# Reordering the hand-over between the two phases of a fused two-layer gated cross-attention kernel on Trainium2

## The reference

```
x = x + tanh(g_xattn[0]) * quantised_matmul(layernorm(x), ctx)           # fp8 steps, context as the weight
x = x + tanh(g_ffn[0])   * ternary_ffn(layernorm(x), W0, gamma)           # RMS norm, 8-bit activations, ternary W0
x = x + tanh(g_xattn[1]) * attention(layernorm(x), ctx, ctx)              # 8 heads of 128 rows per batch, softmax over 1024
x = x + tanh(g_ffn[1])   * mixture(layernorm(x), router_w, Wa, Wb)        # 8 experts of rank 128, the best 2
```

```
scale = max(max(abs(rms_norm(x) * gamma)), 1e-5);  q = round(clip(x / scale * 127, -128, 127))
```

## Time and profile before

| | before |
|---|---|
| median of 3 runs | 2047.13 us (2046.15 to 2052.06) |
| the profiled execution | 2047.11 us, span 2045.3 us |
| granted TensorE clock, mean | 0.982 of full speed |
| TensorE busy | 1859.9 us (91%) |
| VectorE busy | 1542.8 us (75%) |
| ScalarE busy | 1269.0 us (62%) |
| GpSimd busy | 775.0 us (38%) |
| DMA moved | 340.50 MB, mean 166 GB/s |

### The profile page before, as it was taken

How to read it: one execution, slowest core, us unless ns; L and a number is a source line. 1 busy time by engine, 2 the same in 40 slices (tenths; PEclk the granted TensorE clock), 3 DMA queues, 4 the chain that set the end, 5 groups by cost and what they waited for, 6 DMA issues and landing times.

```text
span 2045.3 us, 26459 instructions
## 1 busy us (share of the span) xinstructions
PE 1859.9 (91%) x8968; PEld 838.5 (41%) x8968; DVE 1542.8 (75%) x2386; ACT 1269.0 (62%) x2045; POOL 775.0 (38%) x1100
## 2 busy tenths in 40 slices
PE   1699999983799999999999999999999999999998
PEld 0244444331244444444444444444444444444443
DVE  8899999887777777777777777777777777777662
ACT  4799898655555665665665555665656565565650
POOL 3556565333333333333333333333333333333320
PEclk9999999997799999999999999999999999999998
DMA  9587877795788788888878888788878878887672
GB/s 212 159 213 200 217 208 186 187 233 167 143 157 161 149 164 167 163 159 168 160 159 167 164 163 159 150 167 162 159 161 164 169 157 161 163 171 160 125 147 58
DMA packets 923975, 340.50 MB, mean 166 GB/s; under 512 B 849728, under 2 KB 898880, under 8 KB 923840
## 3 DMA queue, kind: packets, MB, share of 16 engines
q1 hardware_dynamic: 923840, 338.81, 78.8%
HBM read 93.36 MB, written 33.55 MB: 62 GB/s over the span
## 4 chain that ended last, share of the span: by engine, by line
DVE 21%; ACT 20%; issue 19%; POOL 10%; PE 7%; DMA 5%; SPq 1%; ACTq 0%; DVEq 0%; POOLq 0%
ACT slot L881 9%; DVE tiny L1570 7%; ACT arena L868 6%; POOL tiny L707 5%; DVE tiny L1216 4%; POOL tiny L705 4%; DVE slot L1575 3%; ACT tiny L860 3%; DMA slot<-slot 2%; DVE arena L1585 2%; DMA probs<-slot 2%; ACT slot L905 2%; DVE slot L1543 2%; PE accs L1059 1%; PE accs L1060 1%
## 5 line engine op out<-in xcount | busy, mean ns | idle before, releaser
L1575 DVE SCALAR_TENSOR_TENSOR slot<-arena,tiny,slot 128x1024 f16<-128x1024 f32 x256 | 328.2, 1283 | 304.2 <-ACT slot L881 304.0
L881 ACT ACTIVATE slot<-arena,tiny 128x1024 f16<-128x1024 f32 x256 | 294.2, 1149 | 173.1 <-POOL tiny L707 158.1
L1079 PE MATMUL sc<-arena,slot 128*128 128x512 f16 x1536 | 372.3, 382 | 20.9 <-ACT arena L868 18.5
L705 POOL TENSOR_SCALAR tiny<-tiny 128x1 f32<-128x1 f32 x256 | 101.0, 394 | 687.0 <-ACT arena L868 687.0
L1570 DVE TENSOR_REDUCE tiny<-sc 128x1 f32<-128x1024 f32 x256 | 306.6, 1207 | 17.5 <-PE sc L1079 16.2
L868 ACT ACTIVATE arena<-sc,tiny,head_tab 128x1024 f32<-128x1024 f32 x256 | 308.6, 1205 | 8.5
L860 ACT ACTIVATE tiny<-tiny,head_tab 128x1 f32<-128x1 f32 x256 | 74.3, 290 | 346.0 <-DVE tiny L1570 346.0
L1079 PEld LDWEIGHTS sc<-arena,slot 128*128 128x128 f16 x1536 | 150.2, 98 | 207.2 <-ACT arena L868 21.2
L1100 PE MATMUL accs<-probs,arena 128*128 128x512 f16 x512 | 195.9, 383 | 18.9 <-issue 16.4
L1059 PE MATMUL accs<-wa_both,slot 128*128 128x512 f16 x512 | 196.6, 384 | 0.0
L1060 PE MATMUL accs<-wa_both,slot 128*128 128x512 f16 x512 | 196.6, 384 | 0.0
(11 more groups left out here) (212 smaller groups left out, 2902.9 us busy)
## 6 DMA issues: line engine op xcount, KB each, us to landing
arena<-in_x SPq DMA_DIRECT2D x32, 512.0 KB, 4.2
x_scratch<-arena SPq DMA_DIRECT2D x32, 512.0 KB, 3.7
slot<-x_scratch SPq DMA_DIRECT2D x32, 512.0 KB, 4.0
slot<-in_ctx SPq DMA_DIRECT2D x32, 512.0 KB, 4.2
out<-arena SPq DMA_DIRECT2D x31, 512.0 KB, 3.4
slot<-in_L_ffn_Wa SPq DMA_DIRECT2D x12, 512.0 KB, 4.7
slot<-in_L_ffn_Wb SPq DMA_DIRECT2D x9, 512.0 KB, 5.0
wb_hi<-in_ctx SPq DMA_DIRECT2D x64, 64.0 KB, 2.4
```

The source lines that it names most:

```text
L881: act.activation(high, full, ACT.Identity, scale=rinv[c % 4][:]).then_inc(s_ph.sem, 1)
L1079: mm = pe.matmul(sc[:, c % 2, h * HALF:(h + 1) * HALF], q[i][:, c * P:(c + 1) * P], k[j][:, h * HALF:(h + 1) * HALF], start=start, stop=stop)
L1575: dve.scalar_tensor_tensor(out=low, in0=full, scalar=rinv[c % 4][:], in1=high, op0=ALU.mult, op1=ALU.subtract).then_inc(s_pl.sem, 1)
```

## The change

It alters only the hand-over and the prologue.

- SyncE, step j = 31: after the x1 loads it loads context tile 0 as well, waits for the store of tile 29, and loads Wb 0 to 2; at j = 32, behind W0's last transpose, Wb 3 to 5. The stores of x1 tiles 30 and 31 leave the loop.
- SyncE after `go`: quantised tiles 0 and 1 are transposed first, then Wb 6 and 7, context tile 1, the stores of tiles 30 and 31, and the chunks. Key 0 is transposed after chunk 1 (behind a wait for all x1 stores), quantised tile 2 after chunk 5, and context tile 2 is loaded after chunk 6.
- ScalarE makes key 0's high part before `go`, ahead of six Wb tiles; Wb 6 and 7 come after the query of tile 0, key 1's high part after chunk 4.
- VectorE does the mean and gamma of tile 0 (`quantise_norm(0)`) before `x1_max(31)`; after `go` only the scaling (`quantise_scale(0)`) is left. Both quantised tiles are rounded before key 0's low part. Wb 3 comes before the first row maximum, Wb 6 and 7 at chunks 2 and 3, quantised tile 2 at chunks 4 and 5, key 1 at chunk 6, Wb 4 and 5 later in turn 1.
- Two Wb tiles have other landing places: Wb 4 lies in the upper part of `wb_lo` that its own low halves fill later, Wb 5 in slot 4; Wb 6 and 7 stay in the array of probabilities.

```diff
@@ -141,8 +141,8 @@
         C = [ring[:, i] for ring in rings for i in range(4)][:C_RING - 1] + [slot[4][:]]
         CQ = lo_hi(rings[2][:, 3])
         RAW = ((slot[11][:], slot[12][:]), (rings[2][:, 2], rings[2][:, 3]))
-        WB_RAW = [XP[25 % X_RING], XP[26 % X_RING], XP[27 % X_RING], XS, slot[4][:]]
-        WB_RAW += [quarters(probs[:].bitcast(F32))[:, i] for i in range(5, KB)]
+        WB_RAW = [XP[25 % X_RING], XP[26 % X_RING], XP[27 % X_RING], XS, rings[2][:, 2], slot[4][:]]
+        WB_RAW += [quarters(probs[:].bitcast(F32))[:, i] for i in range(6, KB)]
 
         def raw(kind, r):
 
@@ -429,16 +429,18 @@
                 if PREP < j <= PREP + KB:
                     turn_w0(j - PREP - 1)
                 if j == TILES - 1:
-                    sp.wait_ge(x1_out.sem, x1_out.at(TILES - 3))
+                    sp.wait_ge(x_q.sem, x_q.at(TILES - 1))
                     for n in range(3):
                         sp.dma_start(X2[n][:], rows(x1_rows, n)).then_inc(xa_in[n].sem, 16)
+                    sp.dma_start(KX[:], rows(c_rows, 0)).then_inc(kx_in.sem, 16)
+                    sp.wait_ge(x1_out.sem, x1_out.at(TILES - 3))
+                    sp.wait_ge(e_sq.sem, e_sq.at(TILES - 5))
+                    for r in range(3):
+                        load_wb(r)
                 if j == TILES:
-                    sp.wait_ge(x1_out.sem, x1_out.at(TILES - 2))
-                    sp.wait_ge(e_sq.sem, e_sq.at(TILES - 2))
-                    sp.wait_ge(x_q.sem, x_q.at(TILES - 1))
-                    for r in range(5):
+                    for r in range(3, 6):
                         load_wb(r)
-                if is_x(j - 1):
+                if is_x(j - 1) and j < TILES - 1:
                     store_x1(j - 1)
                 if SUM_FROM - 1 <= j < SUM_FROM + KB:
                     load_sum(j - SUM_FROM + 1)
@@ -447,11 +449,6 @@
                 if PREP + 1 <= j < PREP - 1 + KB:
                     load_prep(j - PREP + 1)
 
-            sp.wait_ge(x1_out.sem, x1_out.at(TILES - 1))
-            sp.dma_start(KX[:], rows(c_rows, 0)).then_inc(kx_in.sem, 16)
-            sp.wait_ge(mm1.sem, mm1.at(TILES - 1))
-            for r in range(5, KB):
-                load_wb(r)
             sp.wait_ge(go.sem, 1)
 
 
@@ -519,14 +516,20 @@
                 sp.dma_start_transpose(blocks(HT), T42).then_inc(h_turned.sem, 16)
 
             turn_quantised(0)
+            turn_quantised(1)
+            for r in range(6, KB):
+                load_wb(r)
             load_k(1)
-            turn_quantised(1)
-            turn_keys(0)
+            for n in range(TILES - 2, TILES):
+                store_x1(n)
             for c in range(KB - 1):
                 turn_probs(0, c)
                 if c == 1:
-                    load_k(2)
-            turn_quantised(2)
+                    sp.wait_ge(x1_out.sem, x1_out.at(TILES - 1))
+                    turn_keys(0)
+                if c == 5:
+                    turn_quantised(2)
+            load_k(2)
             for n in range(1, TILES + 2):
                 before, prev, cur, nxt, quant = (is_x(n + d) for d in (-2, -1, 0, 1, 2))
                 if prev:
@@ -799,6 +802,10 @@
                 act.wait_ge(wp_in[r % 2].sem, wp_in[r % 2].at(r // 2))
                 act.activation(raw(0, r), raw(0, r), ACT.Identity, scale=winv[:]).then_inc(w_n.sem, 1)
                 act.activation(wa_hi[:, r, :], raw(1, r), ACT.Identity, scale=wamp[:, 0:1]).then_inc(wa_hi_set.sem, 1)
+
+            def key_high(n):
+                act.wait_ge(kx_in.sem, kx_in.at(n))
+                act.activation(KHL[n % 2][0], KX[:], ACT.Identity, scale=head_tab[:, n, 0:1]).then_inc(k_hi.sem, 1)
 
             def output_high(r):
                 act.wait_ge(wb_in[r].sem, wb_in[r].at(0))
@@ -847,13 +854,10 @@
                 if is_x(j - 1) and j < PREP:
                     x1_square(j - 1)
 
-            for r in range(5):
+            key_high(0)
+            for r in range(6):
                 output_high(r)
             act.wait_ge(go.sem, 1)
-
-            def key_high(n):
-                act.wait_ge(kx_in.sem, kx_in.at(n))
-                act.activation(KHL[n % 2][0], KX[:], ACT.Identity, scale=head_tab[:, n, 0:1]).then_inc(k_hi.sem, 1)
 
             def exp(n, c):
                 act.wait_ge(s_mx.sem, s_mx.at(n, c + 1))
@@ -919,12 +923,10 @@
                 act.wait_ge(m_turned.sem, m_turned.at(n))
                 act.copy(T4HL[0][:, half], T4[:, half]).then_inc(h_hi.sem, 1)
 
-            key_high(0)
-            for r in range(5, KB):
-                output_high(r)
-            key_high(1)
             for h in range(2):
                 query_half(0, h)
+            for r in range(6, KB):
+                output_high(r)
             exp(0, 0)
             for c in range(1, KB):
                 exp(0, c)
@@ -933,6 +935,8 @@
                     query_full(1)
                 if c == 2:
                     query_high(1)
+                if c == 4:
+                    key_high(1)
             prob_high(0, KB - 1)
             for n in range(1, TILES + 1):
                 prev, cur, nxt = (is_x(n + d) for d in (-1, 0, 1))
@@ -1422,6 +1426,26 @@
                 x_mask(n)
                 x_step(n)
                 x_add(n)
+
+            def quantise_norm(n):
+                dve.wait_ge(xa_in[n % 3].sem, xa_in[n % 3].at(n // 3))
+                if n == 0:
+                    dve.wait_ge(x_hi.sem, x_hi.at(TILES - 1))
+                    dve.wait_ge(x_lo.sem, x_lo.at(TILES - 1))
+                    dve.wait_ge(gamma_in.sem, gamma_in.at(0))
+                if n > 1:
+                    dve.wait_ge(l3_lo.sem, l3_lo.at(n - 1))
+                dve.scalar_tensor_tensor(out=Y[n == 1][:], in0=X2[n % 3][:], scalar=row_tab[:, n, 0:1], in1=gamma_b[:],
+                                         op0=ALU.add, op1=ALU.mult).then_inc(s2_y.sem, 1)
+
+            def quantise_scale(n):
+                y = Y[n == 1]
+                dve.wait_ge(s2_y.sem, s2_y.at(n, 1))
+                dve.tensor_scalar(y[:], y[:], row_tab[:, n, 1:2], ROUND_INT, ALU.mult, ALU.add).then_inc(s2_y.sem, 1)
+
+            def quantise_full(n):
+                quantise_norm(n)
+                quantise_scale(n)
 
             dve.wait_ge(ids.sem, 4)
             dve.tensor_reduce(own_block.rearrange("p (n k) -> p n k", k=KB),
@@ -1474,6 +1498,8 @@
                     round_x(j + 2)
                 if is_x(j + 4) and j + 4 >= X_EARLY:
                     x_stats(j + 4)
+                if j == TILES + 1:
+                    quantise_norm(0)
                 if is_x(j - 2):
                     if j == 2:
                         dve.wait_ge(gsq.sem, 1)
@@ -1520,16 +1546,6 @@
             dve.wait_ge(w_turned.sem, w_turned.at(KB - 1))
             dve.tensor_copy(gmax[:], gq[:]).then_inc(go.sem, 1)
 
-            def quantise_full(n):
-                y = Y[n == 1]
-                dve.wait_ge(xa_in[n % 3].sem, xa_in[n % 3].at(n // 3))
-                if n != 1:
-                    after(dve, l3_lo, n - 1)
-                dve.scalar_tensor_tensor(out=y[:], in0=X2[n % 3][:], scalar=row_tab[:, n, 0:1], in1=gamma_b[:],
-                                         op0=ALU.add, op1=ALU.mult).then_inc(s2_y.sem, 1)
-                dve.wait_ge(s2_y.sem, s2_y.at(n, 1))
-                dve.tensor_scalar(y[:], y[:], row_tab[:, n, 1:2], ROUND_INT, ALU.mult, ALU.add).then_inc(s2_y.sem, 1)
-
             def quantise_round(n):
                 dve.wait_ge(s2_y.sem, s2_y.at(n, 2))
                 if n != 1:
@@ -1645,31 +1661,31 @@
                 dve.scalar_tensor_tensor(out=x[:, cols], in0=accs[:, bank, :], scalar=ocol[:], in1=x[:, cols],
                                          op0=ALU.mult, op1=ALU.add).then_inc(o_x4.sem, 1)
 
-            quantise_full(0)
+            quantise_scale(0)
             quantise_round(0)
             quantise_full(1)
+            quantise_round(1)
             key_low(0)
-            quantise_round(1)
             for r in range(2):
                 output_low(r)
             for h in range(2):
                 finish_x2_half(0, h)
             output_low(2)
             finish_x2(1)
+            output_low(3)
             row_maxima(0, 0)
             row_maxima(0, 1)
-            output_low(3)
             for c in range(2, KB):
                 row_maxima(0, c)
                 prob_low(0, c - 2)
-                if c == 2:
+                if c < 4:
+                    output_low(c + 4)
+                if c == 4:
+                    quantise_full(2)
+                if c == 5:
+                    quantise_round(2)
+                if c == 6:
                     key_low(1)
-                if 3 <= c < 6:
-                    output_low(c + 2)
-                if c == 6:
-                    quantise_full(2)
-                if c == 7:
-                    quantise_round(2)
             prob_low(0, KB - 2)
             for n in range(1, TILES + 2):
```

(6 more changed lines are left out.)

## The result

Over five runs the changed kernel took 2032.83 us in the median (2028.76 to 2035.89), the kernel before 2046.15 (2044.05 to 2052.06) in the same rounds: ratio 0.9928 with a 95% interval of 0.991 to 0.9946, **13.3 us faster**. The profiled execution took 2032.83 us, span 2031.0. Of the changed kernel's nine runs (these five and the four of "The changed kernel again") three took 2028.28 to 2029.48 us at a mean granted clock of 0.990, and six 2032.83 to 2036.23 us at 0.987; both profiles of it are from the six.

What follows compares the result with a forecast made beforehand. Bound: the chain of waits between the phases, before a loop of 46.9 us turns where TensorE is nearly always busy. 9.1 - 0.4 + 3.1 + 2.6 = 14.4 us off 2047.1 gives 2032.7 us; 8-in-10 range 2028.5 to 2040.

Steps and rivals of the forecast that it cites:

- Landing of tile 0's transpose: SyncE's queue before product 0: issued at 467.05, landing at 471.4 instead of 480.47, 9.1 us earlier; bounds 7 and 10.
- The bound "empty queue": Upper bound for tile 0's transpose: with nothing queued ahead it lands at 470.97 or a little faster, 10 us gained.
- The first exponential, 0.4 late: ScalarE, tile 0: Wb 6 and 7, about 1.1 us each, into 1.83 us of idle, delay it by 0.4 us.
- Leg 2: Chunks of tile 0: tile 2's earlier transpose starts product 2 3.1 us earlier, the kept clock saves 2.6; bounds 0 and 6.5.
- leg 1: Hand-over before product 0: tile 0's transpose no longer waits for tile 31's store and lands 9.1 us earlier.
- "the clock falls 2 us after the last matmul": TensorE before product 2: the idle dropped the clock to 1.2 GHz; without it 16 matmuls take 3.47, not 6.11 us.
- "What is late next": Second half of tile 0's values: TensorE waits about 1 us for chunk 7, ends at 537.8; VectorE needs it from 539.9.
- A (a gap stays ahead of product 2): Tile 2's transpose lands over 2 us after the scores, the clock falls; gain 9 to 12 us, 2035 to 2038; chance 0.27.
- B (late scale): W0's last transpose, behind seven loads, lands at 467 to 468, delaying the scale 1.6 to 2.5 us: 2035; chance 0.1.
- C (worse rhythm): Loop: turns settle slower at the router's wait; 0.46 us more a turn eats the gain, 0.7 gives 2054; chance 0.04.
- D: Before tile 0's transpose: the wait only changes place, leaving under 6 us of gain, 2041 to 2047; chance 0.05.
- E: Loop: fewer turns over 46.9 us; a third less of 9.5 us of excess gives 2029.5; chance 0.06.

Runs made afterwards that it cites:

- The changed kernel again: The changed kernel run once more with nothing altered: 2034.66 us, ratio 0.994 (0.9917 to 0.9962), hand-over 87.4 us.
- Late mean: The changed kernel with tile 0's mean and gamma (1.28 us) put back behind the scale: one time of 2037.38 us, hand-over 87.2 us.
- the run with the stores first and no wait: The changed kernel with x1 tiles 30 and 31 stored inside the loop again, no wait before tile 0's transpose: 2036.29 us, hand-over 88.8 us.
- The run with extra matmuls: The changed kernel with matmuls whose results are overwritten unread, put where TensorE idles: 2027.74 us, ratio 0.9915 (0.9899 to 0.9932), hand-over 82.8 us.
- leg 2 only: The kernel before with only tile 2 quantised at chunks 4 and 5 and transposed after chunk 5: 2042.48 us, ratio 0.9981, hand-over 99.5 us.
- leg 1 only: The changed kernel with tile 2's quantising and transpose, key 1 and context tile 2 at their old places: 2035.05 us, ratio 0.9944, hand-over 88.7 us.
- late tile 2: The changed kernel with SyncE transposing quantised tile 2 after chunk 6 instead of after chunk 5: one time of 2032.52 us, hand-over 87.11 us.
- context tile 2 early: The changed kernel with context tile 2 loaded after chunk 4's transpose instead of after chunk 6's: one time of 2037.34 us, hand-over 86.15 us.
- before with extra matmuls: The kernel before with matmuls whose results are overwritten unread in its own idle stretches: 2043.49 us, ratio 0.9982 (0.9969 to 0.9995), hand-over 100.25 us.

## Why the prediction was right, step by step

The forecast was 14.4 us and 2032.7; measured are 13.3 us of hand-over, 14.3 of span and 13.3 in the medians. The span has 0.33 us from a phase one that ended earlier and 0.68 from the loop and the end, which is within what single executions differ by there. The mechanism is the one forecast: both gates were where I had put them, and both opened. That the sum comes so close is luck in part, because its errors cancel:

| step of the prediction | forecast | measured | from |
|---|---|---|---|
| tile 0's transpose lands, product 0 starts earlier | 9.1 | 10.3 | 22.88 - 12.55 |
| from product 0 to the first row maximum | -0.4 | -1.8 | 12.58 against 14.38 |
| product 2 starts earlier, from the first row maximum | 3.1 | 3.7 | 36.75 against 33.08 |
| product 2 at the high clock | 2.6 | 2.65 | 6.21 against 3.56 |
| from the add on product 2 to the router | 0 | -1.6 | 21.99 against 23.55 |

*Landing of tile 0's transpose: mis-sized by 1.2 us.* The issue was right: 6.0 us earlier, counted from the last add, against 6.1. The landing behind it took 3.06 us and not the 4.35 that I had from the full queue's pace of 1.55 us a load (471.4 - 467.05). In the changed kernel Wb 3 to 5 landed about 1.25 us apart, and the engines had nothing left to move from 466.8. Late mean shows the other side: one instruction of 1.28 us more before the issue, product 0 later by 1.4. Why the pace of before was slower stays open. A store at its end is not enough: in the run with the stores first and no wait, Wb 4 and 5 landed 1.3 us apart with a store behind them. The bound "empty queue" was the right value.

*The first exponential, 0.4 late: wrong in its cause, and the way there is 1.8 longer.* Wb 6 and 7 took ScalarE 2.18 us and were finished 0.7 us before the row maximum was. What came late was TensorE: products 0 and 1 started at the low clock and kept it longer than before (9.42 against 8.62 us), and then the first scores ran at it too (4.42 against 3.05). I had counted the clock where it falls in the kernel before, and not where it might newly fall in the changed one. The run with extra matmuls has 7.08 and 3.05 us there.

*Leg 2: right in place and in size up to product 2, but not at the router.* The gate was the transpose of tile 2, the clock followed, and the add on product 2 came 6.3 us earlier against 5.7. At the router, counted from the first row maximum, leg 2 alone shows 3.6 us and the whole change 4.8; put on top of leg 1, it shortened the hand-over by 1.6 us. I had split the sum into 8.7 and 5.7 us, and leg 1 alone gave 11.7. But "the clock falls 2 us after the last matmul" does not hold: late tile 2 kept it across 2.56.

*"What is late next": wrong in its size, and the largest error.* I wrote that TensorE waits a microsecond for chunk 7 and that VectorE does not want `values(0, 1)` yet. TensorE waited 2.77 us, the clock then fell and the product took 7.0 us, and VectorE idled 1.46 us for it. Chunk 7's transpose was issued at 518.10 behind `load_k(2)` and took 3.66 us to issue. With that load elsewhere the product starts behind 0.38 us and the hand-over is 1.0 shorter; with product 2 later (late tile 2) the idle is gone as well. The two transposes share one queue: against late tile 2, product 2 starts 2.5 us earlier, counted from the first row maximum, and 1.1 of them reach the router.

*Rivals.* A (a gap stays ahead of product 2) did not occur in the changed kernel; leg 1 only shows what it looks like. B (late scale): the transpose of W0's last tile landed after 8.3 us, at 463.5 instead of the 465.55 I had, 1.7 us ahead of the end of the scale, and its issue took 1.28 us and not the 3.7 that the rival needs; the 2035 that I had hung on ring order did not come. One store more, and the scale waits. The Trainium skill's page on DMA (DMA: Bandwidth & Descriptors, Queues, rings and completion order) has descriptors consumed in ring order: the traces agree, 5.4 us behind four transfers, 8.3 behind seven, 10.1 to 10.2 behind eight. C (worse rhythm): 47.22 us a turn in the changed kernel, 47.15 to 47.26 in all profiles. Nothing moved there; only the turn ahead of these is longer, 48.5 against 47.4 us between the first two `rows_low`, and the sum of loop and end has made that good. D and E did not occur.

## What to carry to other kernels

A wait for a store's landing in front of an issue queue holds everything behind it, and the transfers released between it and a gating transpose can cost more than the wait itself (5.9 against 2.7 us here). Move the store behind what the critical engine needs, and ask of each transfer ahead of a gating transpose whether it must be there. When a reordering shortens a stretch, ask for each TensorE burst in it which clock it will have, the ones that were fast before too; where TensorE must idle for a known time, matmuls without use can be worth more than one more step of reordering (4.3 us against 1.0 for context tile 2 early, here). Judge an edit of a few microseconds by distances inside the profile, cut at places that the edit can't touch, and look at more than one execution.

## What the runs showed of the hardware

- The clock after an idle stretch is not a matter of its length alone: product 2 ran at the high clock behind idles of 2.43 and 2.56 us, and at the low one behind 2.09 and 2.62 us. The same two products started 12.55 to 12.57 us after the last add in five profiles and took 8.93 to 9.63 us. The Trainium skill (TensorE: Matmul & The Clock Gate, What's actually happening) says that one kernel shows different numbers of slow matmuls from run to run; these profiles agree.
- A store of 512 KB behind five loads landed after 8.6 to 11.2 us (8.64 in before, 8.7 in leg 2 only, 11.2 in before with extra matmuls). Product 0 came 22.9 to 25.0 us after the last add in the three profiles with the order of before up to there, and 12.55 to 12.57 us in the five with the changed one (12.45 with extra matmuls). Both transfers ahead of it scatter: in before with extra matmuls the store landed 2.5 us later, in leg 2 only tile 0's transpose, behind its four loads, took 8.3 instead of 7.3 us. In the changed order neither the wait nor these loads are there.
- The issue of a DMA on SyncE can take longer when the queue is full: W0's last transpose took 1.28 us behind seven transfers (and Wb 3 behind it 2.66), 5.11 us with one store more. I can't say from these runs what limit it meets.
